# Queries stored once instead of twice, and each 24-row load of them made as two loads

## What is computed

```python
q = (x @ Wq.T).reshape(b, t, 16, 8); k = x @ Wk.T; v = x @ Wv.T        # k and v: one head of 8
logits = jnp.einsum('btnh,bsh->bnts', q, k) / np.sqrt(8)
masked = jnp.where(jnp.abs(pos[:, None] - pos[None, :]) <= 32, logits, -1e30)
probs = softmax(masked)
out = jnp.einsum('bnts,bsh->btnh', probs, v).reshape(b, t, 128)
x = x + out @ Wf.T + bf
# before and after it: x = x + 0.5 * ffn(layernorm(x)), 16 experts, top 4, plus a shared one
```

## Time and profile before

| | us |
|---|---|
| median of 3 runs | 293.48 |
| lowest and highest | 291.27, 295.85 |
| the profiled execution | 292.86 |
| its span, first to last instruction | 291.1 |
| PE busy | 269.6 (93%) |
| DVE busy | 187.0 (64%) |
| ACT busy | 150.7 (52%) |
| POOL busy | 120.4 (41%) |

### The profile page before, as it was taken

One profiled execution on the slowest core, in us unless ns is written; L12 is line 12 of the kernel. 1 busy time (PEld: TensorE's weight loads), 2 busy tenths in 40 slices (PEclk: granted clock), 3 DMA queues, 4 the chain that ended last, 5 costly groups with the idle time before them and its releaser, 6 DMA issues.

```text
span 291.1 us, 4514 instructions
## 1 busy us (share of the span) xinstructions
PE 269.6 (93%) x1316; PEld 175.7 (60%) x1316; DVE 187.0 (64%) x564; ACT 150.7 (52%) x281; POOL 120.4 (41%) x108
## 2 busy tenths in 40 slices
PE   8998989999999997899899489998999999999995
PEld 3676846565677653466566266466666666766661
DVE  4778964987654357767588267844695796694231
ACT  4775456345234512786677557786635725633320
POOL 5600096942999066350401200005323724680760
PEclk9999999999999999999999689999999999999999
DMA  6800895694439596476667812107100801801911
GB/s 191 268 5 7 252 179 149 207 147 134 160 97 313 120 199 158 83 186 145 133 180 157 136 34 60 31 7 244 45 3 24 268 0 42 269 22 42 286 40 36
DMA packets 44689, 36.82 MB, mean 127 GB/s; under 512 B 19744, under 2 KB 33144, under 8 KB 44664
## 3 DMA queue, kind: packets, MB, share of 16 engines
q1 hardware_dynamic: 43384, 36.39, 48.2%
q10 hardware_dynamic: 1280, 0.13, 0.4%
HBM read 31.71 MB, written 4.84 MB: 126 GB/s over the span
## 4 chain that ended last, share of the span: by engine, by line
PE 45%; DVE 16%; DMA 15%; issue 10%; ACT 7%; POOL 3%; SPq 3%; DVEq 0%; ACTq 0%; POOLq 0%
PE pY L1023 12%; DMA c_all<-comb_dram 4%; DMA q_t<-max_t 4%; PE pU L1094 3%; DVE neg_max L824 3%; PE pG L943 3%; PE pG L1079 3%; PE pU L943 3%; PE pU L945 3%; PE pU L944 3%; POOL ring L473 3%; PE pG L945 3%; PE pG L944 3%; DMA k_diag<-k_dram 2%; PE pY L1107 2%
## 5 line engine op out<-in xcount | busy, mean ns | idle before, releaser
L473 POOL TENSOR_TENSOR ring<-ring,c_all 128x512 f32<-128x512 f32 x57 | 71.9, 1287 | 48.3 <-DMA c_all<-comb_dram 42.4
L787 DVE TENSOR_TENSOR ring<-ring,pU 128x512 f32<-128x512 f32 x64 | 43.6, 683 | 39.6 <-PE pU L945 27.6
L548 ACT ACTIVATE ring<-pG 128x512 f32<-128x512 f32 x64 | 37.9, 597 | 57.3 <-PE pG L945 56.9
L1023 PE MATMUL pY<-ring,wd_sb 128*128 128x512 f32 x128 | 64.7, 598 | 1.2 <-POOL ring L473 1.1
L943 PE MATMUL pG<-xt_hi,wg_hi 128*128 128x512 f32 x72 | 46.1, 640 | 1.9 <-ACT ring L548 1.9
L584 ACT ACTIVATE probs<-pU 128x512 f32<-128x512 f32 x64 | 34.8, 596 | 15.5 <-PE pU L1094 14.2
L458 POOL TENSOR_TENSOR rstd<-var_eps,half 128x4 f32<-128x4 f32 x8 | 8.1, 1011 | 77.6 <-DVE var_eps L691 77.6
L824 DVE TENSOR_REDUCE neg_max<-pG 128x8 fp32r<-128x768 f32 x32 | 30.6, 956 | 12.7 <-PE pG L1079 12.5
L1023 PEld LDWEIGHTS pY<-ring,wd_sb 128*128 128x128 f32 x128 | 22.6, 189 | 11.2 <-issue 6.3
L943 PE MATMUL pU<-xt_hi,wu_hi 128*128 128x512 f32 x72 | 28.8, 400 | 0.4 <-DVE ring L787 0.2
L945 PE MATMUL pG<-xt_lo,wg_hi 128*128 128x512 f32 x72 | 28.4, 395 | 0.0
(11 more groups left out here) (135 smaller groups left out, 439.8 us busy)
## 6 DMA issues: line engine op xcount, KB each, us to landing
c_all<-comb_dram SPq DMA_DIRECT2D x64, 256.0 KB, 4.4
q_stage<-q_dram SPq DMA_DIRECT2D x16, 192.0 KB
q_t<-q_dram SPq DMA_DIRECT2D x16, 192.0 KB
k_diag<-k_dram SPq DMA_DIRECT2D x32, 72.0 KB
q_dram<-q_hi SPq DMA_DIRECT2D x8, 256.0 KB, 3.9
X<-x SPq DMA_DIRECT2D x4, 256.0 KB, 3.9
q_t<-qrows_dram SPq DMA_DIRECT2D x2, 512.0 KB
q_dram<-q_lo SPq DMA_DIRECT2D x4, 256.0 KB, 4.2
```

The lines of the kernel that those rows point to most:

```text
L473: pool.tensor_tensor(ring_at(n), ring_at(n), c_all[:, n % CH], ALU.mult)\
L548: act.activation(ring_at(n), pG[:, n % 2], ACT.Silu).then_inc(silu_done, 1)
L787: dve.tensor_tensor(ring_at(n), ring_at(n), pU[:, n % 2], ALU.mult).then_inc(gu_done, 1)
L1023: pe.matmul(pY[:, u % 2], wd_sb[:, D * e:D * (e + 1)], ring_at(n), start=e == 0, stop=e == CH - 1)\
```

## The change

`q_dram` holds 16 rows per head (hi, lo) instead of 24 (hi, hi, lo), so `store_q` stores q_hi once. The rows in SBUF stay as they were, hi, hi, lo: each load of `q_stage` and of `q_t` is now made as two, one of the first 8 rows (hi) and one of all 16 rows (hi, lo) behind them. The semaphore counts follow.

```diff
--- before.py
+++ after.py
@@ -216,7 +216,7 @@
         p0, p1 = ps("p0", [P, SEQ]), ps("p1", [P, SEQ])
 
         comb_dram = nc.dram_tensor("comb_dram", (2, E, SEQ), F32, kind="Internal").ap()
-        q_dram = nc.dram_tensor("q_dram", (2, NH, PARTS, SEQ), F32, kind="Internal").ap()
+        q_dram = nc.dram_tensor("q_dram", (2, NH, 2 * HD, SEQ), F32, kind="Internal").ap()
         k_dram = nc.dram_tensor("k_dram", (2, PARTS, KROW), F32, kind="Internal").ap()
 
         mask32_dram = nc.dram_tensor("mask32_dram", (32, 3, W32), F32, kind="Internal").ap()
@@ -306,12 +306,11 @@
                 dst = q_dram[a % 2]
                 if a >= 2:
                     for g in (G4 * a - 6, G4 * a - 5):
-                        sp.wait_ge(q_t_in[g % 2], 16 * (g // 2 + 1))
+                        sp.wait_ge(q_t_in[g % 2], 32 * (g // 2 + 1))
                 sp.wait_ge(q_hi_done, a + 1)
                 sp.dma_start(dst[:, 0:HD], q_hi[:].bitcast(F32)).then_inc(q_stored, 16)
-                sp.dma_start(dst[:, HD:2 * HD], q_hi[:].bitcast(F32)).then_inc(q_stored, 16)
                 sp.wait_ge(q_lo_done, a + 1)
-                sp.dma_start(dst[:, 2 * HD:3 * HD], q_lo[:].bitcast(F32)).then_inc(q_stored, 16)
+                sp.dma_start(dst[:, HD:2 * HD], q_lo[:].bitcast(F32)).then_inc(q_stored, 16)
 
             def store_k(a):
                 dst = k_dram[a % 2, :, PAD:PAD + SEQ]
@@ -333,19 +332,21 @@
                         .then_inc(k_diag_in[h], 16)
 
             def load_q_stage(a):
-                sp.wait_ge(q_stored, 48 * (a + 1))
+                sp.wait_ge(q_stored, 32 * (a + 1))
                 wait(sp, q_rep_done, 2 * a)
                 rows = q_dram[a % 2].rearrange("(c j) r t -> j r c t", j=4)
                 for j in range(4):
-                    sp.dma_start(q_stage[PARTS * j:PARTS * (j + 1)].bitcast(F32), rows[j]).then_inc(q_stage_in, 16)
+                    sp.dma_start(q_stage[PARTS * j:PARTS * j + HD].bitcast(F32), rows[j, 0:HD]).then_inc(q_stage_in, 16)
+                    sp.dma_start(q_stage[PARTS * j + HD:PARTS * (j + 1)].bitcast(F32), rows[j]).then_inc(q_stage_in, 16)
 
             def load_q_t(n):
                 a, g = divmod(n, G4)
-                sp.wait_ge(q_stored, 48 * (a + 1))
+                sp.wait_ge(q_stored, 32 * (a + 1))
                 if n > 1:
                     sp.wait_ge(st_psum, 4 * (n - 1))
-                sp.dma_start(q_t[0:PARTS, n % 2].bitcast(F32), q_dram[a % 2].rearrange("h r t -> r h t")
-                             [:, :, P * g:P * (g + 1)]).then_inc(q_t_in[n % 2], 16)
+                heads = q_dram[a % 2].rearrange("h r t -> r h t")[:, :, P * g:P * (g + 1)]
+                sp.dma_start(q_t[0:HD, n % 2].bitcast(F32), heads[0:HD]).then_inc(q_t_in[n % 2], 16)
+                sp.dma_start(q_t[HD:PARTS, n % 2].bitcast(F32), heads).then_inc(q_t_in[n % 2], 16)
 
             def load_k_t(a, g):
                 sp.wait_ge(k_stored, 48 * (a + 1))
@@ -480,7 +481,7 @@
                     .then_inc(bias_added, 1)
 
             def spread_q(a, h):
-                pool.wait_ge(q_stage_in, 64 * (a + 1))
+                pool.wait_ge(q_stage_in, 128 * (a + 1))
                 if a > 0:
                     pool.wait_ge(s_psum, 2 * (G4 * (a - 1) + 2 * h + 2))
                 pool.tensor_copy(q_rep[0:4 * PARTS, h].rearrange("p b c q -> p c b q"),
@@ -566,7 +567,7 @@
 
             def q_high(a):
                 act.wait_ge(q_psum, a + 1)
-                wait(act, q_stored, 48 * a)
+                wait(act, q_stored, 32 * a)
                 act.activation(q_hi[:], p0[:], ACT.Copy).then_inc(q_hi_done, 1)
 
             def kv_high(a):
@@ -1085,7 +1086,7 @@
                 a, g = divmod(n, G4)
                 b, heads = divmod(i, 2)
                 if i == 0:
-                    pe.wait_ge(q_t_in[n % 2], 16 * (n // 2 + 1))
+                    pe.wait_ge(q_t_in[n % 2], 32 * (n // 2 + 1))
                     pe.wait_ge(k_t_in[g], 16 * (a + 1))
                     pe.wait_ge(m_in[n % 2], 16 * (n // 2 + 1))
                 if n == 0 and i == 0:
```

## The result

The kernel with the change takes 315.12 us (median of 6 runs, 310.13 to 316.67), beside 293.12 us before on the same chip (6 runs): a ratio of 1.070 [1.063, 1.077], 22 us slower. The profiled execution took 314.94 us (its span 313.1), against 292.86 and 291.1 before. The forecast was 311.

A forecast was written before the change was run, and what follows sets the result against it. The DMA queue, with q_stage the largest thing in it, was taken to set the chain. q_stage would land 3.9, 10.1, 13.2 and 18.0 us late in units 0 to 3; 18.5 was taken: 292.9 + 18.5 = 311 us, range 296 to 321.

The forecast's parts named there:

- Part (1): Stores of q: one less per unit, -0.95 us of queue and about 0.65 us of SP's issuing.
- Part (2): SP's issuing: 1.8 us more per unit, hidden by the queue; without that cover, 1.2 us once before k_diag.
- Part (3): q_stage and q_t loads: halves run one after the other, 2.4 us a pair where one load cost 1.2.
- near 110: Sign that the forecast is right: DMA rate near 110 GB/s instead of 160 while q_stage loads.
- rival C: q_stage and q_t halves overlap in part; queue content 21.2 us, just the old period; +4 to +5, 297; chance 0.12.
- the queue no longer runs empty and itself is the period: Units 2 and 3: queue content of 26.0 us is more than the unit took, so it sets the period.
- The clock: TensorE's clock in units 1 and 2: longer stalls may lower it; nothing in the sum, up to 3 us in range.
- Behind the last q_stage: Unit 3: k_diag unchanged, q_t of tile 10 +1.2 us; key_scores there about 19 us late.
- Tiles 12 to 15: Last tiles: no further loss; a q_t lands 4.8 us after issue, issued nearly two 4.5 us tiles ahead.
- A: Split loads: the engines are the limit and the halves cost as much as the whole; about 292; chance 0.15.
- B: As A, and a max_t load issued among the halves finds half the queue ahead; 287; chance 0.06.
- D: q_stage pairs: engines running ahead collide with others writing the previous load; 1.2 us in each unit, about 315; chance 0.15.

The follow-up runs named there:

- the second experiment: Kernel before, three stores and 24 rows in DRAM kept, each q_stage and q_t load made as two, of 8 and 16 rows: 314.18 us, ratio 1.076.
- first: Kernel before, each q_stage and q_t load made as two of all 24 rows, half of the heads in each: 291.65 us, ratio 0.996.
- third: Kernel before, three stores kept, each q_stage and q_t load made as two, of 12 and 12 rows: 309.58 us, ratio 1.052.

## Why the prediction was right or wrong

**The direction and the cause were right.** The split is what costs (the second experiment has it alone), it is the rows and not the number of transfers (first against third), and the row that decided it was the one with busy engines and 88 GB/s. The Trainium skill, "SBUF — State Buffer", section "Door 1: The DMA port swizzle", speaks of groups of four neighbouring partitions behind one port, and the load on every third partition agrees: it reaches more of these groups and flows at 230 GB/s. That doesn't prove the rule, since the count of a load's rows alone would give 221 (32 times the 6.9 of the prediction). Why few neighbouring rows are slow stays argued; that they are is shown.

**Part (1), the store:** -0.95 us per unit were counted, and nothing came of it. It was subtracted from a queue that isn't the limit where the store stands; the second experiment pays it and loses the same 22.0 us against the kernel before.

**Part (2), SP:** right. Eight halves take SP from 115.83 to 118.59, 0.69 us a pair (0.75 forecast), and the split by columns shows that they are hidden.

**Part (3), the price of a pair:** oversized in units 1 to 3. Taken was the upper bound, 2.4 us; 1.7 to 2.0 us is what the rates make in the q_stage stretches, and 0.4 to 0.7 above one load for a lone q_t. In unit 0 the price came out: 4.9 us more from issue to cast, where 4.8 were forecast. The prediction didn't agree with itself here: 196.6 kB in 2.4 us are 82 GB/s, yet it named "near 110" as the sign. The sign was right and the price wrong. 110 GB/s is 1.8 us a pair, the price of rival C.

**The sum landed close by two errors that cancel.** Casts were forecast at 108.1, 128.0, 154.0 and 180.0, and came at 108.4, 125.3, 152.3 and 180.8. The step that failed is "the queue no longer runs empty and itself is the period". The DMA share was to be near 0.9 from 127 on; it was 0.83 and 0.72 in the windows by unit, 0.14 from 128 to 130 and 0.42 from 158 to 164. By C's prices the content of a unit is 21.2 us, and the periods were 27.1 and 28.5. What makes a period is a loop: q_stage lands, cast, scores, key_scores behind its q_t, SP issues the next q_t, behind it the stores and the next q_stage. Each thing in it that gets longer adds its length, although the queue has room. In the table, 13.2 us come from issue to cast and 8.2 from the rest of the loop. This is also why C had the right price and the wrong time (297): it charged the excess to a gap in the queue that isn't there to be used.

**The clock:** "nothing in the sum" failed. It costs 2.5 us in unit 2, since the queue doesn't cover PE there; it waits for PE. In unit 1, where the prediction saw the risk too, it costs at most the 0.5 us of the table's row. The forecast had up to 3 us in its range for it. At the last first cast it is already in the 18.8 us (18.0 forecast), where the oversized price of a pair makes up for it.

**Behind the last q_stage:** k_diag and q_t of unit 3 were to bring +1.2 us; it was 2.65 more from the cast to key_scores of tile 10. The cast to the scores of tile 12 went from 2.85 to 3.50, and the scores to key_scores from 0.91 to 2.91. The way from 18.5 to 21.7 is then 0.8 at the cast, 1.45 here, 0.7 that the prediction left off (18.0 + 1.2 is 19.2, and it took 18.5), and 0.2 behind tile 10.

**Tiles 12 to 15:** right. 21.5 us at tile 10, 21.7 at tile 15.

**Rivals.** A and B need the halves to cost what the whole did; the second and third experiments exclude that. C: above. D is supported in part: 2.6 us for the order of the pairs, against the 4.8 that it was given. The result, 315, is D's number exactly, and the total alone would have named D as the explanation. The runs don't bear that out: what the order brings is about half of that, and it stands in the sum together with a cheaper pair, a dearer loop and the clock. That the forecast of 311 lies so near is therefore luck in part.

## What to carry to other kernels

A narrow load is priced by the rows that it writes at a time, not by its bytes alone: before splitting one by rows, compare its GB/s with a wide load's. If rows must be split, try dealing them out over the partitions (every third here, in wide loads) instead of in blocks; here that cost nothing. When a queue's content is set against a period, look whether the loop that feeds it (landing, compute, permission to issue) is longer; if so, each added latency counts in full while the queue still shows idle time. A landing moved earlier may bring nothing where the same landing moved later costs all of it.

## What the runs showed of the hardware that was not expected

- Transfers to neighbouring blocks of partitions overlap in part: 2.0 us for 8 and 16 rows and 2.6 for three times 8, where one load of 24 takes 1.3 to 1.6 (each with a k_t load behind it).
- Splitting a load by columns is free in time on the DMA engines (6.4 us from issue to cast, against 6.9), although it doubles the transfers.
- Where loads of 24 neighbouring rows flow at 165 GB/s, one of 96 rows reaches 237, and three of 32 interleaved rows 230; but an issue of every third row takes SP 0.6 to 0.7 us.
- PE's stalls of 3.58 and 1.89 us were followed by some 6 us at half clock, and in these DMA stood idle for over half of the time, as SP's issues waited for PE.
